# Layer 2 experts: the index products' rounds between the products of the up projection's second half

## The reference

```python
scores = softmax(xf @ gate_w.T); topk_w, topk_idx = top_k(scores, 6)
# the tokens of each expert, up to 64 (CAP) of them, in token order
buf_tok = full((64, 64), T).at[sorted_e, pos].set(sorted_tok, mode='drop')
gx = xp[buf_tok]                                   # gather rows
gu = einsum('ech,ehi->eci', gx, gate_up_proj)      # 256 -> 2 x 96, per expert
hid = silu(g) * u
eo = einsum('eci,eih->ech', hid, down_proj) * buf_w[..., None]
routed = zeros.at[buf_tok].add(eo)                 # scatter back
x = x + 0.5 * (routed + shared)
```

## Time and profile before

| what | us |
|---|---|
| times of three runs | 2366.07, 2353.83, 2366.43 |
| median | 2366.07 |
| the profiled execution | 2379.67 |
| its span, first to last instruction | 2377.9 |
| `l2_ffn_a`, from up(0) to the end of down(7) | about 103 |
| `l2_ffn_b`, the same | about 102 |

### The profile page before, as it was taken

How to read it: one execution, slowest core, us unless ns; L and a number is a source line. 1 busy time by engine, 2 the same in 40 slices (tenths; PEclk the granted TensorE clock), 3 DMA queues, 4 the chain that set the end, 5 groups by cost and what they waited for, 6 DMA issues and landing times. The chain is left out here.

```text
span 2377.9 us, 52407 instructions
## 1 busy us (share of the span) xinstructions
PE 1959.3 (82%) x21293; PEld 1347.6 (57%) x21293; DVE 1212.3 (51%) x3208; ACT 835.6 (35%) x1973; POOL 469.8 (20%) x544
## 2 busy tenths in 40 slices
PE   7984779896999887656899999999998796559568
PEld 3542654565777554433666766766767655336445
DVE  6657541443564337624566666666665156252541
ACT  1012321221552222223576576676674022300120
POOL 0002410331000333631121221221220025500200
PEclk9997989896999998767899999999998887769679
DMA  4000000531500516741010010010000156450000
GB/s 156 0 6 9 1 5 1 161 143 37 213 1 7 176 48 192 254 160 48 20 39 21 21 39 21 21 39 20 21 21 3 36 157 211 137 165 3 10 6 19
DMA packets 55235, 157.39 MB, mean 66 GB/s; under 512 B 12803, under 2 KB 29785, under 8 KB 50726
## 3 DMA queue, kind: packets, MB, share of 16 engines
q1 hardware_dynamic: 43014, 126.74, 15.7%
q0 software_dynamic: 9888, 25.20, 3.3%
q10 hardware_dynamic: 2096, 2.10, 0.4%
HBM read 115.36 MB, written 40.48 MB: 66 GB/s over the span
## 5 line engine op out<-in xcount | busy, mean ns | idle before, releaser
L2165 PE MATMUL l_heads_ps_p<-xnT,l_heads_w 128*128 128x512 f32 x512 | 253.5, 620 | 8.3 <-DMA l_heads_w<-in_l_w_heads 8.3
L2565 DVE SCALAR_TENSOR_TENSOR l_heads_taps<-l_heads_padded,l_heads_conv,l_heads_taps 128x1024 f32<-128x1024 f32 x144 | 182.7, 1279 | 9.2 <-ACT l_heads_taps L2391 8.5
L2165 PEld LDWEIGHTS l_heads_ps_p<-xnT,l_heads_w 128*128 128x128 f32 x512 | 88.4, 191 | 79.9 <-issue 64.0
L206 PE MATMUL norm_turn<-zeros,ident 128*128 128x512 f32 x120 | 68.0, 724 | 57.1 <-PEq L60 57.1
L2740 POOL TENSOR_TENSOR l_heads_e<-l2a_table,l_heads_row 128x512 f32<-128x512 f32 x32 | 33.3, 1042 | 387.2 <-DVE l_heads_first L2576 382.3
L197 ACT ACT_TABLE_LOAD x10 | 12.8, 1283 | 245.3 <-PEq L60 245.3
L578 POOL TENSOR_TENSOR l_qkv_by_sin<-l_qkv_raw,l_qkv_angle 128x512 f32<-128x512 f32 (+1 forms) x16 | 23.2, 1451 | 314.3 <-ACT l_qkv_raw L566 310.9
L379 PE MATMUL l_ffn_a_ps_w<-l_ffn_a_term,ident 128*128 128x512 f32 x240 | 76.8, 473 | 8.6 <-DVE l_ffn_a_term L477 8.6
L206 PEld LDWEIGHTS norm_turn<-zeros,ident 128*128 128x128 f32 x120 | 27.0, 234 | 92.6 <-issue 92.6
L2391 ACT ACTIVATE l_heads_taps<-l_heads_ps_p,l_heads_conv 128x512 f32<-128x512 f32 x96 | 76.0, 792 | 0.0
L2390 ACT COPY l_heads_padded<-l_heads_ps_p 128x512 f32<-128x512 f32 x96 | 56.5, 589 | 50.9 <-PE l_heads_ps_p L2165 50.8
(11 more groups left out here) (694 smaller groups left out, 4898.6 us busy)
## 6 DMA issues: line engine op xcount, KB each, us to landing
l_results<-zeros SPq DMA_DIRECT2D x24, 512.0 KB, 6.3
l_ffn_a_w_in<-in_l_in_w SPq DMA_DIRECT2D x8, 1536.0 KB
l_ffn_b_w_in<-in_l_in_w SPq DMA_DIRECT2D x8, 1536.0 KB
l_heads_w<-in_l_w_heads SPq DMA_DIRECT2D x16, 512.0 KB
l_heads_row<-l_rows SPq DMA_DIRECT2D x16, 512.0 KB
l_ffn_a_w_out<-in_l_out_w SPq DMA_DIRECT2D x8, 768.0 KB
l_ffn_a_w_in<-l_results SPq DMA_DIRECT2D x8, 768.0 KB, 7.9
l_ffn_b_w_out<-in_l_out_w SPq DMA_DIRECT2D x8, 768.0 KB
```

The costliest lines, as they stand in the source:

```text
L206: pe.matmul(turn[:, i % KC, (i // KC) % HALVES, :], core.ident[:], core.zeros[:, 0:HALF], start=True, stop=True)
L2165: mm = pe.matmul(ps_p[half][:], w[b][:, which, c, :], core.xnT[:, c, half * HALF:(half + 1) * HALF], start=(c == 0), stop=(c == KC - 1))
L2565: dve.scalar_tensor_tensor(out=taps[which][:], in0=padded[which][:, :, j:j + SEQ], scalar=conv[p % 2][:, which, j:j + 1], in1=taps[which][ ...
```

## The change

The eight rounds of index(g + 2) no longer follow up(g) as one series. The loop of up(g) draws one round after each of the eight products of its second half (q = 2 and 3). The two waits for `found_ready` and `hot_ready` move with them: they stand now between the halves of up(g), ahead of q = 2. `up_filled` is incremented by the same product as before, the last of q = 1 and of q = 3, and the last round follows that one. Groups 6 and 7 have no rounds, and index(1) ahead of the loop stays one series.

```diff
--- before.py
+++ after.py
@@ -1,3 +1,4 @@
+import itertools
 import math
 from contextlib import ExitStack
 
@@ -3008,17 +3009,23 @@
                                        parts[:, i, 2 * q:2 * q + 2, :].rearrange("p j i -> p (j i)"), start=(i == 0), stop=(i == TILES - 1))
                     mm.then_inc(i_filled, 1)
 
-            def index(g):
-
+            def index_waits(g):
                 pe.wait_ge(found_ready, count_of(g - 1))
                 pe.wait_ge(hot_ready, hot_count(g, PAIRS - 1))
+
+            def index_round(g, i):
+                for q in range(PAIRS):
+                    e = g * EG + 2 * q
+                    mm = pe.matmul(bank_l[ROWS * q:ROWS * q + 6, 0:P], parts[:, i, e:e + 2, :].rearrange("p j i -> p (j i)"),
+                                   hot[g % 2][:, q, i].rearrange("p j s -> p (j s)"),
+                                   start=(i == 0), stop=(i == TILES - 1), tile_position=(0, ROWS * q))
+                if i == TILES - 1:
+                    mm.then_inc(i_filled, 1)
+
+            def index(g):
+                index_waits(g)
                 for i in range(TILES):
-                    for q in range(PAIRS):
-                        e = g * EG + 2 * q
-                        mm = pe.matmul(bank_l[ROWS * q:ROWS * q + 6, 0:P], parts[:, i, e:e + 2, :].rearrange("p j i -> p (j i)"),
-                                       hot[g % 2][:, q, i].rearrange("p j s -> p (j s)"),
-                                       start=(i == 0), stop=(i == TILES - 1), tile_position=(0, ROWS * q))
-                mm.then_inc(i_filled, 1)
+                    index_round(g, i)
 
             def turn_i(g):
                 pe.wait_ge(i_copied, g)
@@ -3039,16 +3046,22 @@
                 b = g % 2
                 pe.wait_ge(w_loaded[g % SETS], 32 * (g // SETS + 1))
                 pe.wait_ge(x_read, KC * (g + 1))
+                rounds = iter(range(TILES if g + 2 < GROUPS else 0))
                 for q in range(PAIRS):
                     if q % 2 == 0 and g >= 1:
                         pe.wait_ge(hidden_ready, 2 * (g - 1) + q // 2 + 1)
+                    if q == PAIRS // 2 and g + 2 < GROUPS:
+                        index_waits(g + 2)
                     for c in range(KC):
                         for j in range(2):
                             e = 2 * q + j
                             mm = pe.matmul(up_of[q // 2][BOTH[j], q % 2, :], xgT[b][:, c, e * S:(e + 1) * S],
                                            w_in[g % SETS][:, e, c, :], start=(c == 0), stop=(c == KC - 1))
-                    if q % 2 == 1:
-                        mm.then_inc(up_filled, 1)
+                            if q % 2 == 1 and c == KC - 1 and j == 1:
+                                mm.then_inc(up_filled, 1)
+                            if q >= PAIRS // 2:
+                                for i in itertools.islice(rounds, 1):
+                                    index_round(g + 2, i)
 
             def turn_h(g):
                 if g >= 1:
@@ -3103,8 +3116,6 @@
             pe.wait_ge(shared_added, TILES // 2)
             for g in range(GROUPS):
                 up(g)
-                if g + 2 < GROUPS:
-                    index(g + 2)
                 turn_h(g)
                 if g + 2 < GROUPS:
                     turn_i(g + 2)
```

## The result

The changed kernel takes 2385.59 us, the median of 4 runs from 2382.15 to 2388.88; before took 2362.55, the median of 4 runs from 2353.83 to 2366.43. The ratio is 1.011, 95% interval 1.0083 to 1.0138: slower by 23.0 us. The forecast was 2385.5, made of 19.4 us on a median of 2366.1 that three runs of before had given; a fourth run moved that median.

What follows compares the result with a forecast made beforehand. No engine was full; a ring of waits, followed at the copy to by_slot, bound the stages. Two stages at 9.7 us gave 19.4, on a median of 2366.1: 2385.5 us, 8-in-10 range 2356 to 2418.

Steps and rivals of the forecast that it cites:

- The step of two changes of division: In up's second half, one up product pair run singly plus one index round and two division changes: 0.60 us, eight 4.8.
- the term for weights that aren't in yet: On PE, the first product after a division change starts before its weights are in: some 0.03 us a step.
- The first copy: DVE's first copy to by_slot in each stage moves from 952.07 to 958.6 in the first stage, 6.5 us later.
- The ring: One_hot, up's second half with rounds, hidden, copy, next one_hot: 12.2 us at the higher clock, 14.3 at the mean clock.
- 3.5 us of lateness: Before's copies waiting for late notices and dragging index series: 35 us over ten intervals, 3.5 each.
- That they go I argue from the rate: Late notices vanish because PE's 96 instructions spread from 1.94 us to 6.9, from 49 a microsecond to 14.
- the sum: Per stage, first copy 6.5 us plus five rounds at 14.3 instead of 13.7, 3.2 us: 9.7, two stages 19.4.
- the case that I named as the way to fail: Late notices exist only in the profiled execution: earlier beat some 11 us, change 30 us or more slower.
- From the profiled execution to the median: The runs' median lay 13.6 us below the profiled 2379.67; the same difference was taken off 2399, giving 2385.5.
- Hidden: Rival: PE's added time vanishes in late notices, or the clock stays high: 2375 or 2360, no difference; chance 0.28.
- Faster: Rival: rounds and up products overlap despite division changes, second half 1.76 us, dragging gone: 2335 or 2350; chance 0.12.
- Late notices that stay whole: Slower case in which each ring is 3.5 us longer, 35 in all: +54 us, 2420; no chance of its own.

Runs made afterwards that it cites:

- e5: Changed kernel with each index product taking 16 experts' parts, in the same array halves as the up products, so no change of division: 2407.38 us, ratio to before 1.0070.
- e9: Changed kernel without layer 2's puts and the waits for them: 2379.60 us, ratio to before 0.9973.
- e8: Kernel before without layer 2's puts and the waits for them: 2332.97 us, ratio to before 0.9791.
- e4: Changed kernel, unedited, profiled and timed again: 2413.70 us, ratio to before 1.0104.
- e10: Kernel before with the index series as 16 products of 256 columns, in the up products' division, instead of 32: 2377.33 us, ratio to before 0.9960.
- e11: Changed kernel with 16 index products of 256 columns, in the up products' division, still interleaved: 2386.58 us, ratio to before 0.9999.
- e1: Kernel before with only the two waits moved between the halves of up, the series staying behind up: 2402.03 us, ratio to before 1.0042.
- e6: Changed kernel with a third buffer of one-hots, filled one group further ahead: 2407.40 us, ratio to before 1.0074.
- e0: Kernel before, unedited, profiled and timed again: 2392.47 us, ratio to before 1.0002.
- e7: Changed kernel with both the same-division index products and the third buffer of one-hots: 2400.13 us, ratio to before 1.0054.

## Why the prediction came out right

**The step of two changes of division**, 0.60 us forecast, 0.63 measured at 2.4 GHz; 1.04 at 1.2 GHz where I had estimated 1.2. The missing 0.03 is mostly the term for weights that aren't in yet: the first instruction behind a change takes 0.377 us and the next 0.326, so 0.05 and not 0.03. e5 shows that the division is the cause. The Trainium skill has it so (TensorEngine Tiling (Array Packing), Key Properties: a change of mode drains TensorE, tiles of one mode run independently), and the trace agrees: 0.63 us with the change, 0.28 without.

**The first copy**, 6.5 us later forecast, 6.6 and 5.9 measured (12.54 and 11.87 us behind up(0), 5.93 and 5.99 before).

**The ring**, 12.2 us at full clock and 14.3 at the mean clock: 12.9 and 13.7 in the first profile, 14.2 and 13.9 in e9, where it stands alone. The forecast had taken over before's granted clock of 0.78; it was 0.89 and 0.84 in the first profile. That before's own ring was 13.7 less 3.5 us of lateness, 10.2, is borne out by e8: 10.6 and 9.7.

**"That they go I argue from the rate"** is the step that failed. In the first profile of the changed kernel they were gone; in e4 they were not, 1.2 to 2.2 us a group, at the gate now and mostly not at the copy. The rate there was 96 instructions in 4.9 us, 20 a microsecond instead of 49, and it did not protect it. The runs show two things in its place. POOL's puts make the most of the lateness: without them (e8, e9) the idle time ahead of the copies is zero, and 1.9 us is the worst at a gate of groups 0 to 6. And what TensorE runs counts: with half the index instructions, in one division, less of it is left (e10, e11). A pause of TensorE ahead of the half seems to help and isn't enough. In the first profile PE had waited 0.4 to 3.4 us for `hot`, and the second gate's notice took 0.04 us in groups 0 to 5, in the midst of the puts too; in groups 2 to 5 of e4 it took 1.5 to 2.2 us where PE had gone through without a pause and still 1.2 where it had stood for 0.2 to 0.7. But in group 1 of e1 PE had waited 2.1 us, and the second gate was 5.3 us late. What in TensorE or its supply of instructions holds a notice back stays open; the unexplained stops between its instructions in e6 and the earlier trace rows speak for the supply, but no run here isolates it.

**Why the sum was still right.** It charged before with 3.5 us of lateness a beat and after with none. In e4 the ring is PE's own, from turn_h to turn_h 1023.05 - 1008.16 = 14.9 us by the timeline, with 1.5 to 2 us of lateness in it and no wait for `hot`; in the first profile it is the ring that I added up. Both lie near 14.3, and the difference to before's 13.7 to 14.4 is small either way. In e4 against e0 the first copies come 7.2 and 5.9 us later and five beats add 5.0 and 1.8, near the 13 and 6.5 of the sum, though the beats don't have the make-up that it gives them. So the total rests more on the first copies and less on the mechanism of the beat than the working says. Between the two kernels without puts (e8, e9) the change costs 46.6 us. Those kernels are not before without its late notices, since POOL's time and other waits go too, but they come nearest to the case that I named as the way to fail. By them, before's late notices hide about half of the change's price.

**From the profiled execution to the median** I subtracted 13.6 us. Before's profiled execution stood 17 above its median and after's 3.4 below, so the forecast of 2399 for a profiled execution was 17 too high. The change of 19.4 us was measured as 23.0, on a median of before that had come out 3.5 lower than the three runs' 2366.1. The two misses cancel, and the hit within 0.1 us is luck; the change itself was forecast 3.6 us too small.

**The rivals.** Hidden: no, the interval excludes no change. Faster: it needed a step under 0.3 us and notices on time. e5 has the first and not the second, and is 17 us slower than before; the bound of 1.76 us for the half was not reached by the kernel as changed. Late notices that stay whole (+54): they stay in part, and largely instead of the wait for `hot`, not on top of it (in e4 PE still waits 6.0 us for it in three groups of the first stage).

**Which part of the change cost what.** The moved waits alone 11 us (e1); the other 12 come with the interleaving, by difference between runs on two chips. Undoing one cost at a time (e5, e6) gives back about 6 each, near the noise, and both 14, clear of it. The 9.7 us that e7 still loses have no run of their own; its trace shows second gates up to 2.3 us late and two second halves of up dragged to 9.7 and 6.9 us. The parts share the late notices and needn't add.

## What to carry to other kernels

Before splitting a series of narrow products among others, look whether they share a division of the array: if not, each visit costs two changes, and the neighbours lose their partners. A wait moved ahead of work that others wait for is paid even when the work itself is free, here half of the loss. And when an engine's successor starts late behind products that had ended, look at what POOL's queue does at that time and count the engine's instructions: fewer and wider ones (in the neighbours' division) gained 10 us here, where moving the same ones lost 23.

## What the hardware showed that I had not expected

TensorE's notices to ACT and DVE can come 1 to 7 us behind the record of the product that gives them (9.8 at worst, in e10), while notices from ACT to DVE in the same stretch take 0.03 us (e1). Where one is late in the middle groups, it is often seen about 0.5 us behind the start of one of POOL's indirect DMAs or about 1.0 us behind the end of the last (1.10 in the rows of e4). Without the puts and the waits for them before is 54.6 us of 2387.61 faster, although POOL itself is busy for only 57 of 103 us in the loops.

The same program ran with a beat of 12.9 us in the first stage of one execution and 14.7 in another, beside medians of before of 2362.55 and 2390.39 us. In the first, PE found time to wait in the middle of up; in the second, its down products ran at the lower clock and in groups 2 to 5 it hardly did.
